# Convolutions written out, a layer norm taken into the MLP, and the weights split early

## What is computed

```
local = batch_norm(depthwise_conv7x7(x))
q, k, v = W_qkv . layer_norm(x) + b;   q = q + layer_norm(local)
y     = x + W_proj . softmax(q k / sqrt(48)) v + b  # 8 heads of 48, all 2304 pixels of an image
z     = layer_norm(depthwise_conv7x7(y) + b)        # "second layer norm"
h     = gelu(W_up . z + b1)                         # 1536 channels
h     = h + grn_g * h * Gx / mean(Gx) + grn_b       # Gx: norm of a channel over an image's pixels
out   = y + W_down . h + b2
```

## Time and profile before

| | us |
|---|---|
| median of 3 runs | 5823.13 (5822.16 to 5826.24) |
| the profiled execution, its own time | 5813.59 |
| its span (first to last instruction) | 5811.8 |
| TensorE busy in the span | 5442.5 (94%) |
| ScalarE, VectorE, GpSimd busy | 3903.1, 3783.7, 2046.2 |

### The profile page before, as it was taken

One profiled execution on the slowest core, in us unless ns is written; L12 is line 12 of the kernel. 1 busy time (PEld: TensorE's weight loads), 2 busy tenths in 40 slices (PEclk: granted clock), 3 DMA queues, 4 the chain that ended last, 5 costly groups with the idle time before them and its releaser, 6 DMA issues. The chain is left out here.

```text
span 5811.8 us, 99229 instructions
## 1 busy us (share of the span) xinstructions
PE 5442.5 (94%) x31248; PEld 5157.1 (89%) x31248; DVE 3783.7 (65%) x5929; ACT 3903.1 (67%) x5612; POOL 2046.2 (35%) x1028
## 2 busy tenths in 40 slices
PE   7879979999999999999999999999888859999999
PEld 7779968999999899999989999999878748989888
DVE  4456658777777677777767777777444464545545
ACT  6755536888888788888878888888537634333333
POOL 0013324555655555555555555556200000000000
PEclk9989988999999999999999999999999979999999
DMA  4467862212131212213131221311465581111111
GB/s 112 119 171 249 264 189 40 37 35 50 30 55 30 55 30 37 48 30 55 30 55 30 36 48 30 55 30 30 147 196 122 120 204 46 58 37 46 46 38 46
DMA packets 653259, 447.99 MB, mean 77 GB/s; under 512 B 482720, under 2 KB 633952, under 8 KB 643424
## 3 DMA queue, kind: packets, MB, share of 16 engines
q1 hardware_dynamic: 547168, 394.38, 28.3%
q10 hardware_dynamic: 105600, 47.51, 3.0%
HBM read 266.88 MB, written 174.59 MB: 76 GB/s over the span
## 5 line engine op out<-in xcount | busy, mean ns | idle before, releaser
L938 POOL TENSOR_TENSOR a_e_lo<-a_e_full,a_e_hi 128x768 fp32r<-128x768 f32 x864 | 1886.2, 2183 | 1402.9 <-ACT a_e_hi L948 1349.2
L1020 DVE TENSOR_REDUCE a_mx_part<-a_ps_m 128x2 f32<-128x768 f32 x1700 | 1628.3, 958 | 747.8 <-PE a_ps_m L1082 718.5
L983 ACT ACTIVATE a_e_full<-a_ps_s 128x768 f32<-128x768 f32 x1728 | 1404.9, 813 | 515.5 <-PE a_ps_s L1100 436.1
L948 ACT ACTIVATE a_e_hi<-a_e_full 128x768 fp32r<-128x768 f32 x1728 | 1450.5, 839 | 0.0
L1100 PE MATMUL a_ps_s<-a_q,a_k_hi 113*128 113x384 f32 x3456 | 1171.7, 339 | 12.6 <-issue 6.7
L1100 PE MATMUL a_ps_s<-a_q,a_k_lo 113*128 113x384 f32 x3456 | 1168.0, 338 | 0.0
L1082 PE MATMUL a_ps_m<-a_k_hi,a_q 112*128 112x384 f32 x3400 | 884.3, 341 | 52.2 <-DMA a_q<-q_lo 36.0
L1114 PE MATMUL a_ps_o<-a_e_hi,a_v 128*97 128x384 f32 x3456 | 919.9, 347 | 8.3 <-ACT a_o_t L954 7.0
L1114 PE MATMUL a_ps_o<-a_e_lo,a_v 128*97 128x384 f32 x3456 | 884.8, 337 | 0.0
L1013 DVE TENSOR_TENSOR a_e_lo<-a_e_full,a_e_hi 128x768 fp32r<-128x768 f32 x864 | 832.8, 964 | 52.4 <-ACT a_e_hi L948 52.4
L1100 PEld LDWEIGHTS a_ps_s<-a_q,a_k_hi 113*128 113x128 f32 x3456 | 651.1, 188 | 36.4 <-issue 9.5
(11 more groups left out here) (150 smaller groups left out, 7235.4 us busy)
## 6 DMA issues: line engine op xcount, KB each, us to landing
local<-c_res ACTq DMA_DIRECT2D x192, 168.0 KB, 2.2
v<-n_v SPq DMA_DIRECT2D x24, 1152.0 KB, 5.8
a_k_hi<-k_hi SPq DMA_DIRECT2D x64, 432.0 KB, 9.6
a_k_lo<-k_lo SPq DMA_DIRECT2D x64, 432.0 KB, 15.9
a_v<-v SPq DMA_DIRECT2D x32, 864.0 KB, 14.4
c_band_raw<-in_taps SPq DMA_DIRECT2D x768, 24.0 KB, 2.3
c_x_raw<-in_x_conv SPq DMA_DIRECT2D x96, 144.0 KB, 2.1
n_xc<-in_x SPq DMA_DIRECT2D x24, 576.0 KB, 6.3
```

What stands on the lines that cost most here:

```text
L938: pool.tensor_tensor(e_lo[:, e], e_full[:, e], f32(e_hi[:, e]), ALU.subtract).then_inc(lo_pool, 1)
L948: act.activation(e_hi[:, slot(par, n)], e_full[:, slot(par, n)], ACT.Copy).then_inc(e_hi_made, 1)
L983: act.activation(e_full[:, slot(par, n)], ps_s[:, n % 2, :, 0:CHUNK], ACT.Exp, scale=float(HD) ** -0.5).then_inc(e_made, 1)
L1020: dve.tensor_reduce(mx_part[:, par, t, 2 * pair:2 * pair + 2], max_bank(h, u), AX.X, ALU.max).then_inc(mx_red[u % 2], 1)
```

## The change

1. `conv_stage`: the loop goes; all 96 groups are written out with constant counts on every engine.
2. `SplitWeights` (new): all weights of qkv and projection are loaded in c0 (three DMAs, 2304 KB), and those of the MLP in c1 (two, 4608 KB), on SyncE behind the third group's loads. They are rounded in cuts of 1152 columns, four in c0 and eight in c1, one every eight groups on ScalarE, with the low part on VectorE a group later. The splits inside qkv, projection and MLP go.
3. Attention: stores and rows of maxima are issued by SyncE; the first head's loads start after the fourth area, on both queues.
4. `norm_stage` goes. The MLP loads c1's result itself (L1275, pieces of 288 bytes, six or nine DMAs a chunk) and does the layer norm of chunk u+1 while chunk u is in work: transposes ahead of f=2, statistics at f=2, the square root behind Gelu(2), normalizing at f=3, transposes back ahead of f=7, 8 and 9, scale and shift behind these Gelus. An image's first chunk is normed in chunks 3 and 4 of "down" of the image before. `m_ps_h` has three slots, and all images are written out.

The diff, cut to its core:

```diff
+class SplitWeights:
+
+    PIECE = 1152
+
+    def __init__(self, nc, held, staged, tag, *sources):
+
+        self.sources = sources
+        widths = [w.shape[1] for w in sources]
+        self.hi = [held.enter_context(nc.sbuf_tensor(f"{tag}_hi{n}", [P, w], F32R)) for n, w in enumerate(widths)]
+        self.lo = [held.enter_context(nc.sbuf_tensor(f"{tag}_lo{n}", [P, w], F32R)) for n, w in enumerate(widths)]
+        self.raw = [staged.enter_context(nc.sbuf_tensor(f"{tag}_raw{n}", [P, w], F32)) for n, w in enumerate(widths)]
+        self.arrived = held.enter_context(nc.semaphore(f"{tag}_arrived"))
+        self.rounded = held.enter_context(nc.semaphore(f"{tag}_rounded"))
+        self.ready = held.enter_context(nc.semaphore(f"{tag}_ready"))
+        self.cuts = [(n, slice(at, at + self.PIECE)) for n, w in enumerate(widths) for at in range(0, w, self.PIECE)]
+
+    def load(self, sp):
+
+        for raw, src in zip(self.raw, self.sources):
+            sp.dma_start(raw[:], src).then_inc(self.arrived, 16)
+
+    def round(self, act, i):
+
+        n, cut = self.cuts[i]
+        if i == 0:
+            act.wait_ge(self.arrived, 16 * len(self.sources))
+        act.activation(self.hi[n][:, cut], self.raw[n][:, cut], ACT.Copy).then_inc(self.rounded, 1)
+
+    def low(self, dve, i):
+
+        n, cut = self.cuts[i]
+        dve.wait_ge(self.rounded, i + 1)
+        dve.tensor_tensor(self.lo[n][:, cut], self.raw[n][:, cut], f32(self.hi[n][:, cut]), ALU.subtract).then_inc(self.ready, 1)
+
+
+def conv_stage(nc, tag, src, taps, affine, dst, beside, nb=B):
...
+    BESIDE_AT = {8 * (i + 1): i for i in range(len(beside.cuts))}
...
-            for g in range(3):
-                body(g, g)
-            with eng.Fori(0, FULL_TURNS) as i:
-                for k in range(TURN):
-                    body(i * TURN + 3 + k, k % 3)
-            for g in range(REST, PG):
+            for g in range(PG):
                 body(g, g % 3)
...
             load(2)
+            beside.load(sp)
             for g in range(3, PG):
                 load(g)
...
-                if not isinstance(g, int) or g >= 1:
+                if g >= 1:
                     finish(g - 1, (k + 2) % 3)
+                if g in BESIDE_AT:
+                    beside.round(act, BESIDE_AT[g])
...
+                if g - 1 in BESIDE_AT:
+                    beside.low(dve, BESIDE_AT[g - 1])
...
+            sp.wait_ge(made_dve, 4)
+            sp.dma_start(f32(k_hi[0:HD, 0]), kh_v[0, 0]).then_inc(q_k_hi_in, 16)
+            sp.dma_start(f32(q[0:HD, 0]), qh_v[0, 0]).then_inc(q_k_hi_in, 16)
+            sp.wait_ge(made_k_lo, 2)
+            sp.dma_start(f32(k_lo[0:HD, 0]), kl_v[0, 0]).then_inc(k_lo_in, 16)
+            sp.dma_start(f32(v[:, 0, :, 0:ROW]), v_v[0, 0]).then_inc(v_in_sem, 16)
+
+            def row(h, half):
+                sp.wait_ge(row_out, h * 2 + half + 1)
+                sp.dma_start(f32(q[MROW:MROW + 1, h % 2, half * (N // 2):(half + 1) * (N // 2)]).rearrange(
+                    "o (t p) -> o t p", p=P), mx_row[:, half]).then_inc(row_in[half], 16)
+
+            def store(h, c):
+                sp.wait_ge(o_made, h * NCH + c + 1)
+                at_least(sp, stored, (h * NCH + c) * 16)
+                sp.dma_start(out_v[h // HEADS, h % HEADS, c], o_tok[:, c % 2]).then_inc(stored, 16)
+
+            row(0, 0)
+            for h in range(NHEAD):
+                if h + 1 < NHEAD:
+                    load(h + 1)
+                if h:
+                    store(h - 1, NCH - 1)
+                row(h, 1)
+                for c in range(NCH - 1):
+                    if c == 3 and h + 1 < NHEAD:
+                        row(h + 1, 0)
+                    store(h, c)
+            store(NHEAD - 1, NCH - 1)
+            sp.wait_ge(stored, NHEAD * NCH * 16)
...
+            act.wait_ge(made_dve, 4)
+            act.dma_start(f32(k_hi[KB:KB + HD, 0]), kh_v[0, 0]).then_inc(q_k_hi_in, 16)
+            act.dma_start(f32(q[KB:KB + HD, 0]), ql_v[0, 0]).then_inc(q_k_hi_in, 16)
+            act.wait_ge(made_k_lo, 2)
+            act.dma_start(f32(k_lo[KB:KB + HD, 0]), kl_v[0, 0]).then_inc(k_lo_in, 16)
...
+        TOK_AT, SD_AT, NORMAL_AT = 2, 2, 3
+        CH_AT = {7: 0, 8: 1, 9: 2}
+        X_AT = {2: 0, 3: 1, 4: 2}
+        NEXT_LN, NEXT_X = 3, 4
+        NEXT_STATS, NEXT_SD, NEXT_NORMAL = {2: 0, 3: 1, 4: 2}, 5, {6: 0, 7: 1, 8: 2}
+        NEXT_CH = {9: 0, 10: 1, 11: 2}
...
+            def raw(u):
+                b, c = divmod(u, NCH)
+                if c:
+                    sp.wait_ge(to_tok, u * 3)
                 if c == 1:
                     at_least(sp, stored, b * NCH * 16)
+                for at, s0, s1, n0, n1 in pieces(c):
+                    for t in range(CT):
+                        sp.dma_start(raw_of(u)[:, t, at:at + (s1 - s0) * (n1 - n0)].rearrange("p (s n) -> p s n", n=n1 - n0),
+                                     src[t * P:(t + 1) * P, s0:s1, b, n0:n1]).then_inc(raw_in, 16)
+
+            def results(b):
...
+            raw(0)
...
+            raw(1)
+            for b in range(nb):
+                if b:
+                    raw(b * NCH + 1)
+                for c in range(2, NCH):
+                    raw(b * NCH + c)
+                results(b)
...
+            def affine(u, t):
+                act.wait_ge(to_ch, u * 3 + t + 1)
+                if t == 0:
+                    at_least(act, x_lo_made, u * CT)
+                act.activation(full[:, t], ps_ln[:, (t + 1) % 2, 0:CHUNK], ACT.Identity, scale=gam[:, t:t + 1],
+                               bias=bet[:, t:t + 1]).then_inc(full_made, 1)
+
+            def deviation(u):
+                act.wait_ge(stats, (u + 1) * 2 * NT)
...
+                        if c + 1 < NCH and f == SD_AT:
+                            deviation(u + 1)
+                        if c + 1 < NCH and f in CH_AT:
+                            affine(u + 1, CH_AT[f])
...
+                    if b + 1 < nb and c == NEXT_LN and f == NEXT_SD:
+                        deviation((b + 1) * NCH)
+                    if b + 1 < nb and c == NEXT_LN and f in NEXT_CH:
+                        affine((b + 1) * NCH, NEXT_CH[f])
+                    if b + 1 < nb and c == NEXT_X and f in X_AT:
+                        x_high((b + 1) * NCH, X_AT[f])
...
+                        if c + 1 < NCH and f == TOK_AT:
+                            for t in range(NT):
+                                statistics(u + 1, t)
+                            moments(u + 1)
+                        if c + 1 < NCH and f == NORMAL_AT:
+                            inverse(u + 1)
+                            for t in range(NT):
+                                normal(u + 1, t)
...
+            def tokens(u):
+                pe.wait_ge(raw_in, landed(u))
+                for t in range(NT):
+                    for c in range(CT):
+                        last = pe.transpose(tok_of(u)[:, t, c * P:(c + 1) * P], raw_of(u)[:, c, t * P:(t + 1) * P], ident[:])
+                    last.then_inc(to_tok, 1)
+
+            def channels(u, c):
+                pe.wait_ge(normed, u * 3 + 3)
+                at_least(pe, full_made, u * 3 + c - 1)
+                for t in range(3):
+                    last = pe.transpose(ps_ln[:, (c + 1) % 2, t * P:(t + 1) * P], nrm_of(u)[:, t, c * P:(c + 1) * P], ident[:])
+                last.then_inc(to_ch, 1)
+
...
+                    if c + 1 < NCH and f == TOK_AT:
+                        tokens(u + 1)
+                    if c + 1 < NCH and f in CH_AT:
+                        channels(u + 1, CH_AT[f])
+                    at_least(pe, h_made, b * NF + n - 2)
...
+                    if b + 1 < nb and c == NEXT_LN and f == TOK_AT:
+                        tokens((b + 1) * NCH)
+                    if b + 1 < nb and c == NEXT_LN and f in NEXT_CH:
+                        channels((b + 1) * NCH, NEXT_CH[f])
...
+            tokens(0)
+            for c in range(CT):
+                channels(0, c)
+            pe.wait_ge(w.ready, len(w.cuts))
```

More of the change, by code:

```diff
@@ L1245, in _ @@
         def _(pe):
-            pe.wait_ge(w_ready, 1)
+            pe.wait_ge(w.ready, len(w.cuts))
             def turn(s, k):
@@ L1420, in up @@
[L1420 to L1424 removed]
+                    u = b * NCH + c
+                    if c:
+                        act.wait_ge(x_free, u)
+                        for t in range(CT):
+                            x_high(u, t)
```

432 lines of the change are left out of this document (146 added, 286 removed).

## The result

The changed kernel takes 5749.7 us (median of 3 runs, 5749.1 to 5760.1) against 5823.1: a ratio of 0.9881 [0.9868, 0.9895], 73 us faster. Measured a second time it took 5739.1 against 5807.2, 68 us, with the same ratio. The forecast had the sign and the range right, and the size wrong: -32 where -68 to -73 came out.

What follows compares the result with a forecast made beforehand. TensorE was seen as nearly always busy in attention and MLP, a two-group load loop as bounding the convolutions. Norm removal (-133) and smaller gains against transposes (+45), border (+32) and convolutions (+42) summed to -32: 5791 us, range 5738 to 5832.

Steps and rivals of the forecast that it cites:

- The transposes: MLP: 46 sets of nine transposes in up and down, +45 us; VectorE's extra work in down's chunks 3 and 4, +3.
- The table loads: MLP up chunks: two more loads each, 1.28 us apiece, cost 0 because Gelu(3) ends 0.6 us before TensorE needs it.
- their rival: Gelu(3) of every up chunk: table loads stop TensorE, +51 us if each is paid, 5842 in all; chance 0.12.
- The starts of qkv and projection: Waits for the weights' rounding and low parts go: -8 us in qkv, -2 in projection.
- The convolutions' sum: Both convolutions: +12 us for weights' transfers, +6 for cuts, +24 for instruction packets, 0 for removed register instructions.
- signs of being wrong: Convolution stages not longer, an up chunk over 23 us, or tokens at the image border waiting under 4 us.
- the first of them: Rival on the convolutions: they do not pay, straight-line fetch is hidden and registers mattered; 5747 us, chance 0.20.
- the fourth: Rival on the convolutions: groups lose 0.4 us each, more than the packets cost; +3 in all, 5826 us, chance 0.08.
- step 1: Attention: moving 192 stores and 64 rows of maxima from ScalarE to SyncE changes 0, with -10 and +10 as ends.
- step 2: MLP: an image's first x is ready when up starts, so today's wait for x_lo goes, -4 us.
- step 3: MLP image borders: nine loads wait for the store of `io`; 8.6 us idle plus 2 slow, three times, +32 us.
- Step 4: Attention's start: first loads follow the fourth memset instead of the seventh, -7.5 us (5 to 10).

Runs made afterwards that it cites:

- d_attend_only: The kernel before with the changed kernel's attention stage and nothing else: 5795.4 us against 5812.6, ratio 0.9974.
- e1_early_load: The changed kernel with the second chunk's load of images 1 to 3 moved two chunks earlier, into the hidden tensor: 5708.8 us, ratio to before 0.9834.

## Why the prediction was right in sign and wrong in size

**Right, by its own steps.** The norm stage's removal (-133, measured -133.5). The transposes (+45 and +3: a chunk 2.03 longer in up, 2.5 in the third chunk of down, 48 in all). The table loads (0, with a cover of 0.6; measured 0, cover 0.4); their rival falls. The starts of qkv and projection within 1.5 us. The convolutions' sum (+42, measured 38.5), if with other parts: the weights' transfers about 15 (forecast 12; the first long groups, 6.3 and 4.4 us in the one and 12.5 and 4.6 in the other instead of 3.1 to 3.4), writing out 14 to 20 (forecast 24), and what is left, 4 to 10, for the cuts (forecast 6), within the few us by which a convolution wanders.

None of the prediction's own signs of being wrong came: the convolutions are longer, an up chunk takes 22.6 us, the tokens wait 6.57. The rivals fall by their mechanisms too, the first of them in spite of its number, and the fourth since the convolutions lost 0.20 us a group, not 0.4.

**Wrong, step 1: attention at 0, for the moved DMAs alone, as "the change leaves the steady part of that alone".** The forecast priced what a loop costs inside the loop. A loop's edge is a cost too, and it depends on code elsewhere: attention became 11 us shorter, 7 to 8 of it at two taken branches whose loop had come to lie elsewhere, as the kernel with nothing but written-out convolutions shows. The other 3 to 4 are in the heads away from the edges and go with attention's own code (`d_attend_only`); what in it does that stays open.

**Wrong, step 2: the MLP's gains were "what it waits for x_lo today goes: -4" and nothing else.** The images were written out as well. The sum has no term for that, and alone it is worth 9.6 us in the MLP. The rows that were read are of the border of images 0 and 1, ahead of the loop; of the two that lie inside it no row was read. The -4 itself was about right: with the border's wait gone (`e1_early_load`) the four chunks 0 take 91.1 us, where those of the kernel before, with four times 2.03 for the transposes, would take 95.8.

**Wrong, step 3: "3 x 10.6 = +32".** The mechanism was right and its size off: 24.5 to 26.5, by the kernel without the wait. TensorE's transposes start 5.9 us after the first of the nine loads is issued, not 7.5, and it is idle for 6.57 us, not 8.6: three times 2 us, 6 in all. The 2 us for the slow matmuls behind the wait were about right.

Steps 2 and 3 make 15 to 17 of the 18 us in the MLP. Another 1.6 are the split of the second weight, which had made the third chunk of the first image 22.2 us long. **Step 4**, small: attention's start gained 10.3, not 7.5, as two queues issue the first loads.

All these errors point one way, which is why they add up to 36 us: the forecast found each cost of the change, took one of them too high, and missed two of its gains.

The rule of the Trainium skill that the forecast set aside ("Runtime: NRT & Kernel Launch", section "Instruction fetch mechanics": a taken branch to code that isn't at hand costs, straight code is mostly hidden) was read for the convolutions alone. There the runs speak against preferring straight code: no packet comes in the loop's later passes, and straight code costs 0.7 to 1 us a packet, beside landings that end last. For the larger loops of attention and MLP they agree with it: written out, these gained some 22 and 12 us, and needed no more packets than as loops (153 and 41 instead of 167 and 47). Against the page "ScalarE: Activation LUTs" of the Trainium skill (section "What ACT_TABLE_LOAD costs", a drain of about 1380 ns with a load) the measurement decides: 0.01 us, in the earlier trace rows and at 4704.85.

## What to carry to other kernels

Writing a loop out is several edits in one: count the instruction packets of the loop's later passes first. Where there are none, as in the convolutions here, straight code adds packets, and they are paid where a DMA ends last; where each pass brings them anew, as in attention, straight code adds none, and the waits at the taken branch go. Read those in a pass inside the loop, not at its first border. Code that gets longer moves every later loop in the instruction stream, and a stage that nobody touched changed here by 7 us. When a store and the next load share a buffer, look whether a part of a larger tensor is already free: here that was worth about 25 us.

## What was not expected of the hardware

The same attention loop cost 112.7 to 113.4 us, 108 to 110 or 102.6 to 104.8 at the head behind a taken branch, and 100 without the branch. With attention's code untouched, longer convolutions ahead of it brought 112.7 to 109.0; but head 11 took 104.8 in one program and 108.3 in another with the same code ahead. The early transfers of weights (2304 and 4608 KB) left the whole kernel at the same time on SyncE's queue at once, on GpSimd's queue some 7 us sooner, and in pieces of 576 KB (5739.1, 5735.7 and 5738.0, each within 4 us of the others).
